# A recurrent attention layer: lane scales transposed on VectorE, SyncE's loads in another order, values 18 steps behind keys in place of 20

## The reference

```
state = state * alpha_t
err   = v_t - state^T k_t
state = state + beta_t * k_t err^T
o_t   = state^T q_t
```

## Time and profile before

| | |
|---|---|
| median of 3 timed runs | 2519.36 us (2518.95 to 2524.99) |
| span of the profiled execution, first to last instruction | 2517.0 us |
| TensorE busy | 2226.2 us, 88% |
| VectorE busy | 1849.5 us, 73% |
| ScalarE busy | 1472.1 us, 58% |
| GpSimd busy | 1086.6 us, 43% |
| DMA engines, hardware queue | 31.7% of 16 engines' span |

### The profile page before, as it was taken

One profiled execution on the slowest core, in us unless ns is written; L12 is line 12 of the kernel. 1 busy time (PEld: TensorE's weight loads), 2 busy tenths in 40 slices (PEclk: granted clock), 3 DMA queues, 4 the chain that ended last, 5 costly groups with the idle time before them and its releaser, 6 DMA issues.

```text
span 2517.0 us, 66167 instructions
## 1 busy us (share of the span) xinstructions
PE 2226.2 (88%) x23576; PEld 1441.3 (57%) x23576; DVE 1849.5 (73%) x2925; ACT 1472.1 (58%) x2755; POOL 1086.6 (43%) x1440
## 2 busy tenths in 40 slices
PE   2486769999999999999999999999988888999998
PEld 2233345655565565555556555565555567777776
DVE  7685667878878787888878878787755556677665
ACT  3475546666666666666666666666655535555554
POOL 1015483654737356383745628365470022222222
PEclk9998889999999999999999999999999999999999
DMA  7546534233333324333332432433232110111100
GB/s 284 161 103 141 125 82 89 75 82 90 86 85 92 85 69 91 87 81 89 93 85 79 93 89 66 94 92 74 68 89 54 42 53 14 31 36 44 32 21 18
DMA packets 500791, 205.37 MB, mean 82 GB/s; under 512 B 437072, under 2 KB 454224, under 8 KB 498512
## 3 DMA queue, kind: packets, MB, share of 16 engines
q1 hardware_dynamic: 500432, 200.76, 31.7%
HBM read 128.33 MB, written 72.35 MB: 80 GB/s over the span
## 4 chain that ended last, share of the span: by engine, by line
PE 57%; issue 12%; ACT 9%; DVE 8%; SPq 8%; DMA 4%; POOL 2%; ACTq 0%; POOLq 0%; DVEq 0%
PE PS L1272 16%; PE PS L1286 10%; PE PS L1350 7%; PE PS L1510 3%; PE PS L1366 3%; DVE Y L1022 3%; PE PS L1439 3%; ACT XN L790 3%; PE PS L1472 3%; PE PS L1323 2%; ACT Y L771 2%; PE PS L1500 2%; PE PS L1458 2%; DMA SCR<-PGD 2%; SPq L377 1%
## 5 line engine op out<-in xcount | busy, mean ns | idle before, releaser
L1022 DVE SCALAR_TENSOR_TENSOR Y<-PS,CW,Y 128x504 f32<-128x504 f32 (+2 forms) x1536 | 1115.6, 732 | 443.2 <-ACT Y L764 391.4
L764 ACT ACTIVATE Y<-PS,CW 128x512 f32<-128x512 f32 x512 | 397.8, 777 | 473.7 <-PE PS L1272 459.3
L1286 PE MATMUL PS<-WOS,XN 128*128 128x256 f16 x3072 | 379.6, 274 | 2.5 <-DVE XN L1037 1.5
L1286 PEld LDWEIGHTS PS<-WOS,XN 128*128 128x128 f16 x3072 | 301.8, 98 | 95.2 <-issue 4.0
L626 POOL TENSOR_TENSOR SQ<-KQ 128x512 f32<-128x512 f32 x128 | 136.0, 1063 | 469.6 <-PE PS L1314 378.4
L1272 PE MATMUL PS<-XK,WH 128*128 128x512 f16 x1024 | 313.9, 389 | 16.3 <-DMA XK<-XHD 16.3
L1272 PE MATMUL PS<-XV,WH 128*128 128x512 f16 x1024 | 310.4, 385 | 8.9 <-issue 8.3
L612 POOL TENSOR_TENSOR SCR<-SCR 128x31 f32<-128x31 f32 (+15 forms) x496 | 290.0, 585 | 38.9
L1350 PE MATMUL PS<-XN,M 64*64 64x256 f32 x2048 | 250.1, 382 | 48.9 <-ACT XN L790 46.3
L609 POOL TENSOR_TENSOR SCR<-SCR 128x31 f32<-128x31 f32 (+15 forms) x496 | 259.4, 523 | 33.0
L790 ACT ACTIVATE XN<-PS,KN 128x256 f32<-128x256 f32 x512 | 212.2, 465 | 63.3 <-PE PS L1286 63.2
(11 more groups left out here) (141 smaller groups left out, 3108.8 us busy)
## 6 DMA issues: line engine op xcount, KB each, us to landing
PGD<-SCR SPq DMA_DIRECT2D x128, 256.0 KB, 2.1
SCR<-PGD SPq DMA_DIRECT2D x128, 256.0 KB, 3.1
EQD<-XN SPq DMA_DIRECT2D x32, 512.0 KB, 4.1
SCR<-EQD SPq DMA_DIRECT2D x128, 128.0 KB, 2.6
SCR<-QND SPq DMA_DIRECT2D x128, 128.0 KB, 3.3
XP<-in_x SPq DMA_DIRECT2D x16, 512.0 KB, 4.9
SCR<-in_wall SPq DMA_DIRECT2D x8, 1024.0 KB, 7.5
SCR<-PGD SPq DMA_DIRECT2D x64, 128.0 KB, 3.2
```

What stands on the lines that cost most here:

```text
L764: A_.activation(Y[:, b, :], PJ[b][:, :], ACT.Identity, scale=CW[:, h[1] % NH, cw0 + 3:cw0 + 4], bias=CW[:, h[1] % NH, cw0 + 4:cw0 + 5]).th ...
L1022: V_.scalar_tensor_tensor(yv[:, :, m:T], pv[:, :, 0:T - m], CW[:, h[1] % NH, cw0 + 3 - m:cw0 + 4 - m], yv[:, :, m:T], ALU.mult, ALU.add).t ...
L1286: ins = mm(VWB[:, E * i:E * i + E], VHL[:, vk, n, P * a:P * a + P], WOS[:, wk, 2 * (w[1] % NH) + n, :], start=(t == 0), stop=(t == 5))
```

## The change

- `AHEAD` goes from 4 to 2: values run 18 steps behind keys. `AT_STEP` becomes 6 steps with one unit, 11 with two, one with none.
- GpSimd's step does the squares first, and the lanes' parts one step earlier (begin at ph 1, rows at ph 2 to 6, end at ph 6).
- beta is transposed once, in 32x32 blocks, on VectorE (BET) and stored so; `load_beta` is then one contiguous load, and waits for an earlier instruction of the lanes.
- The key norms KNL are transposed straight into KN on VectorE, at ph 6 (`lane_scales`), in place of a store to DRAM (KND) and four loads. ScalarE's `values` and GpSimd's begin wait for `kn_done`.
- SyncE: `load_values` is split. EN and T1 are loaded for head v+2 when that is even (`load_pair`), the Grams for head v+1 (`load_gram`). `store_lanes` moves from ph 0 to ph 7 of the step before; the wait for its landing from ph 1 to ph 0. For batch 0, the store, the wait and head 0's loads stand together in the last step with v = None.

```diff
-AHEAD = 4
+AHEAD = 2
-        AT_STEP = [1] * 8 + [2] * 10 + [0, 0]
+        AT_STEP = [1] * 6 + [2] * 11 + [0]
# SyncE, step(v, k)
-                if ph == 1 and exists(back(k, 17)):
-                    sp.wait_ge(S["st_le"], batches(back(k, 17), 48, 48))
+                if v is not None and ph == 0 and exists(back(k, 16)):
+                    sp.wait_ge(S["st_le"], batches(back(k, 16), 32, 32))
                 if v is None and k[1] == NH + AHEAD - 1:
-                    stored_eq(UNITS)
-                    load_values((0, 0))
+                    store_lanes((0, 0))
+                    sp.wait_ge(S["st_le"], at(32))
+                    load_pair((0, 0))
+                    load_gram((0, 0))
                 if exists(v):
-                    v1 = (v[0], v[1] + 1)
+                    v1, v2 = (v[0], v[1] + 1), (v[0], v[1] + 2)
+                    if exists(v2) and v2[1] % 2 == 0:
+                        load_pair(v2)
                     if exists(v1):
-                        load_values(v1)
+                        load_gram(v1)
...
-                if ph == 0 and exists(back(k, 16)):
-                    store_lanes(back(k, 16))
+                if v is not None and ph == 7 and exists(back(k, 15)):
+                    store_lanes(back(k, 15))
# SyncE, load_beta
-                for q in range(4):
-                    src = BED[32 * q:32 * q + 32].rearrange("i (b l) -> b i l", l=BL)[ds(g * 2 + off // 8, 1)]
-                    sp.dma_start(BLN[32 * q:32 * q + 32, :], src.rearrange("o i l -> (o l) i"),
-                                 allow_slow_non_contiguous=True).then_inc(S["ld_bl"], 16)
+                src = BED.rearrange("p (b i) -> b p i", i=BL)[ds(g * 2 + off // 8, 1)]
+                sp.dma_start(BLN[:, :], src.rearrange("o p i -> (o p) i")).then_inc(S["ld_bl"], 16)
# GpSimd, step(v, k)
-                if exists(kb):
-                    if ph == 2:
-                        lanes_begin(kb)
-                    if ph >= 2:
-                        for j in range(JCUT[ph - 2], JCUT[ph - 1]):
-                            lanes_row(kb, j)
-                    if ph == 7:
-                        lanes_end(kb)
                 if exists(back(k, 1)):
                     squares(back(k, 1))
+                if exists(kb):
+                    if ph == 1:
+                        lanes_begin(kb)
+                    if 1 <= ph <= 6:
+                        for j in range(JCUT[ph - 1], JCUT[ph]):
+                            lanes_row(kb, j)
+                    if ph == 6:
+                        lanes_end(kb)
# VectorE
+            V_.transpose(BET, BEA.rearrange("p g h a -> p (g h a)")).then_inc(S["gate_v"], 1)
...
+            def lane_scales(k):
+
+                dve.wait_ge(S["lane"], batches(k, LANE_OPS, 5))
+                if after(k, 16):
+                    dve.wait_ge(S["vw_ev"], heads(back(k, 8), 2))
+                dve.nop(nofuse=True)
+                V_.transpose(KN[:, (k[1] // 8) % 2, :], KNL[:, :]).then_inc(S["kn_done"], 1)
...
+                if k[1] % 8 == 6 and exists(back(k, 14)):
+                    lane_scales(back(k, 14))
```

More of the change, by code:

```diff
@@ L355, in load_xv, with load_pair @@
                 sp.dma_start(XV[:, :, :], XHD[ds(g + off // NH, 1)].rearrange("o p c t -> (o p) c t")).then_inc(S["ld_xv"], 16)
-            def load_values(w):
+            def load_pair(w):
                 g, off = w
                 b = ds(g * 2 + off // 8, 1)
-                s = off % 2
[L362 to L366, removed]
-                    for q in range(4):
[L368 to L378, removed]
-                    if after(w, 4):
-                        sp.wait_ge(S["m_done"], heads(back(w, 2)))
-                        sp.nop(nofuse=True)
-                    for n in range(2):
-                        src = QND[b].rearrange("o p i -> (o p i)").rearrange("(l n t) -> n l t", n=2, t=T)[n, l0:l0 + 8, :]
-                        sp.dma_start(T1[u][64 * n:64 * n + 64, :, :], src[None, :, :].broadcast_to([T, 8, T])).then_inc(S[f"ld_t{u}"], 16)
@@ new lines, in load_pair @@
+                u = (off // 2) % 2
+                l0 = 4 * (off % 8)
+                if after(w, 4):
+                    sp.wait_ge(S["nu_mm"], heads(back(w, 2)))
+                    sp.nop(nofuse=True)
+                for q in range(4):
+                    sp.dma_start(EN[u][32 * q:32 * q + 32, :, (q % 2) * 32:(q % 2) * 32 + 32],
+                                 ED[b, 32 * q + l0:32 * q + l0 + 8, :].rearrange("o l (j i) -> (o j) l i", j=BL)).then_inc(S[f"ld_en{u}"], 16)
+                if after(w, 4):
+                    sp.wait_ge(S["m_done"], heads(back(w, 2)))
+                    sp.nop(nofuse=True)
@@ L385, in load_values, with load_gram @@
+                for n in range(2):
+                    src = QND[b].rearrange("o p i -> (o p i)").rearrange("(l n t) -> n l t", n=2, t=T)[n, l0:l0 + 8, :]
+                    sp.dma_start(T1[u][64 * n:64 * n + 64, :, :], src[None, :, :].broadcast_to([T, 8, T])).then_inc(S[f"ld_t{u}"], 16)
+            def load_gram(w):
+                g, off = w
+                s = off % 2
                 if after(w, 2):
@@ L387, in load_values @@
                     sp.nop(nofuse=True)
-                sp.dma_start(PGVF[s], PGD[b, :, off % 8, :].rearrange("o p x -> (o p) x")).then_inc(S[f"ld_pv{s}"], 16)
+                sp.dma_start(PGVF[s], PGD[ds(g * 2 + off // 8, 1), :, off % 8, :].rearrange("o p x -> (o p) x")).then_inc(S[f"ld_pv{s}"], 16)
             def spill(k):
@@ L426, in load_beta @@
                 if after(k, 8):
[L427 removed]
+                    sp.wait_ge(S["lane"], batches(back(k, 8), LANE_OPS, 7))
                     sp.nop(nofuse=True)
[L429 to L432 removed]
+                src = BED.rearrange("p (b i) -> b p i", i=BL)[ds(g * 2 + off // 8, 1)]
+                sp.dma_start(BLN[:, :], src.rearrange("o p i -> (o p) i")).then_inc(S["ld_bl"], 16)
             def store_lanes(k):
@@ L584, in lanes_begin @@
                 pool.wait_ge(S["ld_lp"], batches(k, 64, 64))
-                pool.wait_ge(S["ld_bl"], batches(k, 64, 64))
+                pool.wait_ge(S["ld_bl"], batches(k, 16, 16))
+                if after(k, 8):
+                    pool.wait_ge(S["kn_done"], batches(k))
                 pool.nop(nofuse=True)
```

21 lines of the change are left out of this document (10 added, 11 removed).

## The result

The changed kernel takes 2535.39 us (median of 5, 2533.13 to 2538.21) against 2519.36: ratio 1.0067, 95% interval 1.0049 to 1.0085, so 0.7% slower. Forecast was 2483 us. The profiled span grew by 14.3 us, from 2517.0 to 2531.3.

The account below looks back on a forecast made before the run. TensorE's own instruction stream was taken as the bound (busy 88% of 2517.0 us). Terms -20.9 + 2.2 + 2.6 + 0 - 20.5 = -36.6 gave a span of 2480.4, timed 2483 us; forecast band 2476 to 2492 (0.52), wider range 2467 to 2505.

Parts of the forecast that it names:

- The loop starts stay: Starts of TensorE's loop body: six, about 1.6 us each without a releaser, about 10 us in all, taken as unchanged.
- term (b): L415 load of 32x32 blocks: lands sooner, squares stalls 19.0 to 10.4 us; low clock 8.4 to 0.5.
- Squares ahead: GpSimd's squares put ahead of the inverse parts: same instruction sequence written out, so worth 0.
- Term (a): Gram load on SyncE: late by 0.9 us only every second batch, stalls 9.0 to 5 us, bounds 0 and 13.
- rival 3: SyncE's wait for the store's landing too long, gram late in all 14 batches: slower, about 2534 us; chance 0.05.
- Rival 1: Stalls stay, GpSimd starts as late as now (8 or more), only the steps go: 2500 us; chance 0.22.
- Key norms on VectorE: 16 transpositions of 128x32 under VectorE's cover: 0, at most 4.5 us.
- earlier keys-only steps: The first 17 keys-only steps, 185.82 us: taken as 0, range -3 to +3.
- Two steps fewer: Pipeline of 146 steps for 148: two values-only steps of 10.47 us go, -20.9; two steps becoming full cost +2.2.
- Keys-only end: End of the keys-only part: stall of 17.03 us covered by a full step, net +2.6 us, bounds -1 to +8.
- the upper bound of 8: Keys-only end, worst case: head 0's own loads come late, TensorE runs dry and returns at low clock, +8 us.

Follow-up runs that it names:

- run 1: Changed kernel with TensorE's loop body placed at slot 0 of a 256-instruction block: 2502.72 us, ratio 0.9940 to the kernel before.
- run 13: Changed kernel with TensorE's loop body at slot 100, nothing else: 2476.01 us, ratio 0.9843 to the kernel before.
- run 2: Kernel before with TensorE's loop body at slot 235, shortly ahead of a block's end: 2537.57 us, ratio 1.0080.
- run 14: Kernel before with TensorE's loop body at slot 100: 2521.22 us, ratio 1.0020.
- run 18: Changed kernel with TensorE's loop body at slot 200: 2512.91 us, ratio 0.9983 to the kernel before.
- run 8: Changed kernel with values again 20 steps behind keys, TensorE's loop body at slot 0: 2505.69 us, ratio 0.9952 to the kernel before.
- run 4: Changed kernel with GpSimd beginning a batch's inverses one step later, behind the third step's squares: 2490.78 us, ratio 0.9892 to the kernel before.
- run 9: Changed kernel with inverses begun one step later, behind the squares, and TensorE's loop body at slot 100: 2456.76 us, ratio 0.9765 to the kernel before.
- run 17: Changed kernel with values again 20 steps behind keys, TensorE's loop body at slot 100: 2484.25 us, ratio 0.9864 to the kernel before.
- run 5: Changed kernel with inverses begun one step later, behind the squares, and TensorE's loop body at slot 0: 2473.01 us, ratio 0.9816 to the kernel before.
- run 7: Kernel before with TensorE's loop body at slot 0: 2532.75 us, ratio 1.0058.
- run 11: Changed kernel with inverses begun one step later, behind the squares, TensorE's loop body at slot 100 and its branch named: 2450.41 us, ratio 0.9740.
- run 15: Changed kernel with TensorE's loop body at slot 100 and its loop-closing branch named: 2470.31 us, ratio 0.9811 to the kernel before.
- run 16: Kernel before with TensorE's loop body at slot 100 and its loop-closing branch named: 2516.51 us, ratio 1.0001.
- run 6: Changed kernel with inverses begun one step later, behind the squares, TensorE's loop body at slot 0 and its branch named: 2457.86 us, ratio 0.9766.
- run 3: Changed kernel with TensorE's loop-closing branch named, body not placed: loop starts of 13.3 to 15.6 us; total not given in the text.

## Why the prediction was wrong

Two steps failed. The first is one sentence: "The loop starts stay." It put a term at nothing that measured +27.4 us. The second is term (b), the landing of the L415 load and the squares stalls behind it, which was to fall by 16.5 us with its share of the low clock and rose by 18.5. Most of both misses has one source: where TensorE's loop body lies in its instruction stream. The change has no edit in TensorE's code; it only takes two keys-only steps out ahead of the loop. Counted in the traces, TensorE has 152 recorded instructions fewer up to its first loop-closing branch (7343 for 7495), and 4627 in a pass in both kernels. The forecast treated instructions as free of place.

- *Loop starts, 0 forecast, +27.4 measured.* Shown by runs 1 and 13 (placing the body brings the steps from 20.5 to about 15.3) and in the kernel before by runs 2 and 14. The prediction also counted six; the branch is taken back five times.
- *Term (b), squares, 10.4 us of idle time and 0.5 of clock forecast; 25.0 and about 21 measured* (46.2 - 25.0). Both went past their bounds, 22 and 8.4. At slot 100 the term is 14.8 and 1.1, so about 30 us are the packet of TensorE's instructions in the middle of the load (runs 13 and 18, and the batches of run 8), and 5 us are a mis-sized part of the sum: the load goes out 2.63 us after the mark with or without the packet, not 2.05. The forecast took 0.55 us from the EQ issue to this load, where the earlier trace rows have 634.75 - 633.58 = 1.17 and the changed kernel 1.09. The clock went past its bound because a stall of 1.6 to 2.6 us with no gram stall ahead of it brought the low clock 11 times in 13, at 1.6 to 2.1 us each.
- *Squares ahead, 0 forecast.* Right: as written it changes no order on GpSimd. Run 4 shows what the real thing is worth: 44 us on the changed kernel, 20 at slot 100 (runs 9 and 13, by the ratios).
- *Term (a), gram, 5 left of 9.0 forecast.* 0.6 left. The order in the sum was right: every second batch is the later one. The forecast had the load 0.3 us in time and 0.9 late; in the trace it lands 2.2 to 4.0 us ahead of TensorE's need in seven batches and 0.2 to 0.7 ahead in six. The store's landing is 2.7 us at the median, as taken. So rival 3 is out, though its 2534 us meets the measured 2535: that is chance. Rival 1's sign, a begin at 8 or more, came in eight of 13 batches, but not for its reason: at slot 100 the same pieces let GpSimd begin at 7.4.
- *Key norms on VectorE and earlier keys-only steps, 0 forecast.* Right: 16 x 203 ns, with no idle time of VectorE put down to them, and the mark of head 16 moved from 305.03 to 305.56.
- *Two steps fewer, -20.9.* -25.0. Before, the first two values-only steps take 14.55 and 12.11 us in place of 10.47 and those stalls go too, less 1.7 us more in the two blocks behind; run 17 gives 20.8 for the two steps alone. The two full steps took 26.28, as reckoned.
- *Keys-only end, +2.6.* The sum up to head 20 is +5.9 for 4.8. The stall forecast to go (17.03) did, but head 0's loads took 6.6 of it back. That is the case of the upper bound of 8, but it cost little.
- *Sum.* At slot 100 the three stretches come to +2.7, -21.5 and -26.9 for +4.8, -20.5 and -20.9, and the time to 2476 for 2483. That is agreement of the sum, and in part luck: within the long stage a smaller gram term and a larger squares term cancel, and slot 100 was not the kernel's own place. The range was too narrow, since no rival held that code ahead of a loop can shift its body.

Why slot 0 gives idle times of 1.5 in one pass and 3.3 in the next can be read from the packets. Of the 100 loop starts in the 20 traces, 11 have a branch of 4.8 to 5.1 us (runs 1, 4, 5, 7 and 8, all at slot 0 or at the changed kernel's own place). In these 11, and in no other, two large packets start close together behind the branch's start, the first at 0.6 to 0.8 us and the second at 0.9 to 1.6. In the others the branch took at most 4.0.

What stays open: where exactly the changed kernel's own body begins. Its packet passes where slot 0's does, and its loop starts are worse than at slot 0 or 235, which speaks for a place just ahead of a block's end; that was not measured. Every placed body also uses another form of the loop call than the changed kernel's own, and no run has that form with neither slot nor named branch. That the slot itself counts rests on the runs that differ in the slot alone: 2, 7 and 14 for loop starts (22.8, 15.5 and 9.2 us over) and squares in the kernel before, 1, 13 and 18 for the squares in the changed one, whose loop starts are alike there (13.7, 11.3 and 13.5).

## What to carry to other kernels

Where the queue view shows instruction packets passing at each start of a loop body, a change of the unrolled code ahead of the loop is two changes: fix the body's slot in both versions before comparing them, and try two or three slots. Here the slot alone moved one kernel by 37 us (slot 200 against slot 100), and by 2.2%, 56 us, against the place that it had by chance (ratios 1.0067 and 0.9843). A stand-still with no releaser ("issue") at a loop start belongs in the sum with a range, and the queue view tells how many packets passed in it. To get work ahead of a late load, read the written-out sequence over the edge of a step: moving both calls left it as it was.

## What the runs showed of the hardware

- TensorE's loop-closing branch, when taken, took 3.6 us at the median in both kernels, and 0.35 us when it was named at the head of the iteration and the body began at slot 100 (all five in each of runs 11, 15 and 16). It took 4.8 to 5.1 us in the 11 passes in which another 16 KB packet of instructions had started just ahead of the one for the branch (run 5: four of five). Naming it left 3.3 to 3.9 us at slot 0 (run 6) and 1.7 to 2.1 at the changed kernel's own place (run 3, four of five).
- A 16 KB packet of instructions, 0.5% of the sixteen DMA engines' time over 10 us (0.8 us of one), held up a load of 4 x 128 KB in short pieces by 0.6 to 1.4 us (begin at 7.91 and 8.72 against 7.36 after the mark).
- With waits for squares of 0.7 to 1.5 us (run 13) TensorE kept its full clock (the step of 14.33 us above is at 1.00). Behind waits of 1.6 to 2.6 us (changed kernel, 12 of them) the clock fell in 11 steps: 0.90 over the step, that is partly 1.2 instead of 2.4 GHz, and 1.6 to 2.1 us on top. With the 5.31 us it was 0.84. The length of the wait does not settle it alone: in run 1 five waits of 1.64 to 1.79 us cost nothing beyond themselves.
